# Forward side work of a mixed transformer and state-space kernel: output products, norm and half the gated unit ahead of the input projection

## What is computed

```python
# block 2, per sequence; h is the conditioned norm of x
xz = h @ in_w;  xs, z = split(xz);  xs = silu(xs)
proj = xs @ xproj_w
dt = softplus(proj[..., :512] + dt_bias);  B, C = proj[..., 512:576], proj[..., 576:]
hst = hst * exp(dt[:, None] * A) + (dt * xs)[:, None] * B     # 64 states, over 256 times
y = sum over states of hst * C + xs * Dskip
out_dir = (y * silu(z)) @ out_w                                # once forwards, once backwards
x = x + gate * (h_fwd + h_bwd)
h, gate = conditioned norm of x
return x + gate * ((silu(h @ mlp_w1) * (h @ mlp_w2)) @ mlp_w3)
```

## Time and profile before

| | us |
|---|---|
| median of the runs | 3309.45 |
| profiled execution | 3316.36 |
| its span | 3314.5 |
| PE, DVE, ACT, POOL busy | 3058.3, 2884.0, 2904.8, 2911.3 |

### The profile page before, as it was taken

One profiled execution on the slowest core, in us unless ns is written; L12 is line 12 of the kernel. 1 busy time (PEld: TensorE's weight loads), 2 busy tenths in 40 slices (PEclk: granted clock), 3 DMA queues, 4 the chain that ended last, 5 costly groups with the idle time before them and its releaser, 6 DMA issues.

```text
span 3314.5 us, 71769 instructions
## 1 busy us (share of the span) xinstructions
PE 3058.3 (92%) x23032; PEld 2760.6 (83%) x23032; DVE 2884.0 (87%) x3203; ACT 2904.8 (88%) x6357; POOL 2911.3 (88%) x1552
## 2 busy tenths in 40 slices
PE   8778999999999999999999999999999999998877
PEld 6568988898888988889888898888888898887766
DVE  2269999899989998899998999899988999989985
ACT  1189999898989989899998999899898989989993
POOL 0069999998999999999998999999999999999995
PEclk6699999999999999999999999999999999999998
DMA  5011111111111111111111111112111111111210
GB/s 179 0 42 45 45 46 54 43 52 44 46 51 45 52 44 47 51 50 44 46 54 44 51 45 45 53 45 52 44 47 50 51 46 45 45 50 44 55 47 26
DMA packets 163039, 162.61 MB, mean 49 GB/s; under 512 B 17610, under 2 KB 156874, under 8 KB 162644
## 3 DMA queue, kind: packets, MB, share of 16 engines
q1 hardware_dynamic: 162644, 157.69, 17.5%
HBM read 154.44 MB, written 3.18 MB: 48 GB/s over the span
## 4 chain that ended last, share of the span: by engine, by line
PE 50%; ACT 23%; issue 11%; DVE 8%; POOL 7%; DVEq 0%; ACTq 0%; POOLq 0%; DMA 0%; SPq 0%
PE ps L1263 13%; ACT dA L584 12%; PE ps L1247 12%; ACT uBT L570 6%; PE ps L1010 6%; POOL hst L417 5%; DVE hst L909 5%; PE ps L1245 4%; PE ps L1082 3%; PE ps L1019 3%; PE ps L1057 3%; PE ps L1066 1%; PE ps L1255 1%; PE ps L1131 1%; POOL uBT L430 1%
## 5 line engine op out<-in xcount | busy, mean ns | idle before, releaser
L417 POOL TENSOR_TENSOR hst<-hst,C_sb 128x1024 f32<-128x1024 f32 x1024 | 2447.3, 2407 | 176.1 <-DVE hst L909 172.7
L909 DVE TENSOR_TENSOR_SCAN hst<-dA,ps 128x512 f32<-128x512 f32 x2048 | 2376.7, 1203 | 146.3 <-PE ps L1263 112.9
L584 ACT ACTIVATE dA<-dt,A 128x255 f32<-128x255 f32 x4096 | 1745.0, 501 | 1.4 <-DVE hst L909 1.2
L1263 PE MATMUL ps<-ident,hst 128*128 128x128 f32 x8192 | 1240.7, 274 | 46.8 <-POOL hst L417 46.7
L1247 PE MATMUL ps<-ident,uBT 128*128 128x128 f32 x7104 | 1084.5, 275 | 52.6 <-DVE hst L909 39.8
L570 ACT ACTIVATE uBT<-uT,BT 128x512 f32<-128x512 f32 x1376 | 936.4, 717 | 117.3 <-PE ps L1247 89.2
L1263 PEld LDWEIGHTS ps<-ident,hst 128*128 128x128 f32 x8192 | 963.2, 141 | 62.9 <-POOL hst L417 62.2
L1247 PEld LDWEIGHTS ps<-ident,uBT 128*128 128x128 f32 x7104 | 844.6, 142 | 195.3 <-DVE hst L909 69.4
L430 POOL TENSOR_TENSOR uBT<-uT,BT 128x512 f32<-128x512 f32 x400 | 427.2, 1068 | 1.4 <-PE ps L1245 1.4
L1245 PE MATMUL ps<-uBT,uT 128*128 128x128 f32 x2176 | 302.7, 284 | 33.9 <-DVE hst L909 27.9
L1245 PEld LDWEIGHTS ps<-uBT,uT 128*128 128x128 f32 x2176 | 272.9, 197 | 45.7 <-DVE hst L909 35.9
(11 more groups left out here) (146 smaller groups left out, 2176.0 us busy)
## 6 DMA issues: line engine op xcount, KB each, us to landing
C_sb<-c_dram SPq DMA_DIRECT2D x1024, 128.0 KB, 2.9
gate_l<-gate_rows_dram SPq DMA_DIRECT2D x16, 256.0 KB, 3.8
x_att<-in_x_dram SPq DMA_DIRECT2D x8, 256.0 KB, 3.6
w<-in_L_cond_W_dram SPq DMA_DIRECT2D x2, 1024.0 KB
out_dram<-x_glu SPq DMA_DIRECT2D x8, 256.0 KB, 3.1
wg<-in_L_cond_mlp_w_dram SPq DMA_DIRECT2D x3, 512.0 KB, 11.0
w_xp<-_L_cond_fwd_xproj_w_dram SPq DMA_DIRECT2D x1, 1280.0 KB, 12.5
w_xp<-_L_cond_bwd_xproj_w_dram SPq DMA_DIRECT2D x1, 1280.0 KB, 14.4
```

The lines of the kernel that those rows point to most:

```text
L417: pool.tensor_tensor(h, h, C_sb[:, n % FED:n % FED + 1, :].to_broadcast([P, KI, NB]), ALU.mult).then_inc(hC_ready.sem, 1)
L584: done = act.activation(dA[:, n % NT, c, lo:hi], dt[:, d, c, lo:hi], ACT.Exp, scale=A[:, d, c, n:n + 1])
L909: dve.tensor_tensor_scan(pair(hst[:, n % NR]), pair(dA[:, n % NT]), ps[:, BANK_U + (2 * n + e) % (2 * NU), :][:, way], 0.0, ALU.mult, ALU. ...
L1263: last = pe.matmul(ps[:, BANK_Y + j, c * P:(c + 1) * P], hst[:, n % NR, c, j * P:(j + 1) * P], ident[:, :], start=False, stop=(n == NS - 1 ...
```

## The change

Only the forward pass changes. The order of its side work becomes: post, norm, glu 0 to 4, ins, dts 0 to 13, then glu 5 to 16 with dts 14 to 20 spread among them, dts 21 to 23, first. The silu of the gated unit moves from its own step (with its two table loads) into ins step 10, in front of the two silu operations there; in the tail after the last pass it keeps its own step. The side work starts at h8 instead of h6. The diagonal states of the forward pass move from 22 to 27 to 30 to 35. PE's waits that guard the two shared PSUM banks and the shared tiles follow the new order.

**Where the steps lie after, batches 1 to 6:** post h8 to h16 (transposes h8, DVE copy h9, products h10 to h13, residual h15); norm 0 to 5 h16, h18, h18, h19, h20, h21; glu 0 to 4 h21, h23 to h26; ins 0 to 11 h26 to h38 (step 8 h35, step 10 h36); dts 0 to 13 h38 to h52; glu 5 to 10 h53, h54, h55, h56, h58, h59; glu 11 to 16 h60, h62, h63, h64, h65, h67; dts 14 to 20 h55, h58, h60, h61, h64, h66, h67; dts 21 to 23 h69, h70, h71; first from h72. In batch 0: dts 17 to 20 at h50, h53, h55, h58. In batch 7: dts 17 to 20 at h106, h111, h115, h117, dts 22 at h122.

```diff
--- before.py
+++ after.py
@@ -43,7 +43,7 @@
     NEG = -1e30
     NR = 4
     BEHIND = 3
-    BY_DIAGONAL = ((1, 3, 22, 23, 24, 25, 26, 27, 61, 63), (1, 3, 55, 57, 59, 61, 63))
+    BY_DIAGONAL = ((1, 3, 30, 31, 32, 33, 34, 35, 61, 63), (1, 3, 55, 57, 59, 61, 63))
     by_pool = lambda d, n: n % 2 == 1 and n in BY_DIAGONAL[d]
     by_act = lambda d, n: sum(not by_pool(d, k) for k in range(n))
     FED = 4
@@ -87,10 +87,8 @@
             first = has_next * (stage("first", "norm") + stage("first", "qkv") + stage("first", "heads0") + stage("first", "heads1", 0, HEADS_BEFORE))
             if not has_prev:
                 return stage("own", "ins") + stage("own", "dts") + first
-            return (stage("own", "ins", 0, 10) + meanwhile(stage("last", "post"), stage("own", "ins", 10, 12))
-                    + stage("own", "dts", 0, 2) + meanwhile(stage("own", "dts", 2, 14), stage("last", "norm", 0, 4))
-                    + stage("own", "dts", 14, 17) + stage("last", "norm", 4, 5) + stage("own", "dts", 17, 18) + stage("last", "norm", 5, 6)
-                    + stage("own", "dts", 18, STEPS["dts"]) + stage("last", "glu") + first)
+            return (stage("last", "post") + stage("last", "norm") + stage("last", "glu", 0, 1 + KG) + stage("own", "ins") + stage("own", "dts", 0, 14)
+                    + meanwhile(stage("last", "glu", 1 + KG, STEPS["glu"]), stage("own", "dts", 14, 21)) + stage("own", "dts", 21, STEPS["dts"]) + first)
         if not has_next:
             return stage("last", "post")
         return (stage("first", "heads1", HEADS_BEFORE, STEPS["heads1"]) + stage("last", "post")
@@ -103,7 +101,7 @@
             self.steps = order(d, has_prev, has_next)
             rooms = [self.room(j) for j in range(len(self.steps))]
             self.behind = [[] for i in range(2 * NS)]
-            start = 2 if d == 1 and has_next else FIRST_HALF + 2 * d
+            start = 2 if d == 1 and has_next else 8 + 2 * d
             end = LAST_HALF[d]
             rest = sum(r for r, step in zip(rooms, self.steps) if step[1][:5] != "heads")
             heads = sum(step[1][:5] == "heads" for step in self.steps) + 1
@@ -501,9 +499,12 @@
                         act.preload_act_table_set(LN_EXP)
                     yield
 
-            def prepare(p, d):
+            def prepare(p, d, gated=None):
                 for i in range(STEPS["ins"]):
                     if i == 2 + 2 * KI:
+                        if gated is not None:
+                            act.wait_ge(glu_raw.sem, glu_raw.at(gated, KG))
+                            act.activation(gT[:, :, :], gT[:, :, :], ACT.Silu).then_inc(glu_silu.sem, 1)
                         act.wait_ge(in_raw.sem, in_raw.at(p, KI + TT))
                         act.activation(xsT[:, :, :], xsT[:, :, :], ACT.Silu).then_inc(in_ready.sem, 1)
                         act.activation(sz[:, d], sz[:, d], ACT.Silu).then_inc(in_ready.sem, 1)
@@ -530,9 +531,9 @@
             def post(p):
                 yield from idle(STEPS["post"])
 
-            def glu(b):
+            def glu(b, alone):
                 for i in range(STEPS["glu"]):
-                    if i == 1 + KG:
+                    if i == 1 + KG and alone:
                         act.wait_ge(glu_raw.sem, glu_raw.at(b, KG))
                         act.activation(gT[:, :, :], gT[:, :, :], ACT.Silu).then_inc(glu_silu.sem, 1)
                         act.preload_act_table_set(LN_EXP)
@@ -549,9 +550,9 @@
                 yield from idle(STEPS["down"])
                 yield from norm(b, LN_SSM)
 
-            def close(b):
+            def close(b, alone):
                 yield from norm(b, LN_GLU)
-                yield from glu(b)
+                yield from glu(b, alone)
 
             def forcing(p, d, n):
 
@@ -605,12 +606,12 @@
                 l0 = layer0(b + 1) if has_next else None
 
                 def own():
-                    yield from prepare(2 * b + 1, 1)
+                    yield from prepare(2 * b + 1, 1, b - 1 if has_prev else None)
 
                 def last(b, d):
                     yield from post(2 * b + d)
                     if d == 1:
-                        yield from close(b)
+                        yield from close(b, False)
 
                 def backward():
                     yield from l0
@@ -643,7 +644,7 @@
             period(NBLK - 1, True, False)
             for _ in post(2 * NBLK - 1):
                 pass
-            for _ in close(NBLK - 1):
+            for _ in close(NBLK - 1, True):
                 pass
 
         @block.vector
@@ -1300,14 +1301,14 @@
                     p = 2 * b + d
 
                     def before(j):
-                        if plan.steps[j] == ("last", "post", 0) and d == 0:
-                            pe.wait_ge(in_raw.sem, in_raw.at(p + 1, KI + TT))
                         if plan.steps[j] == ("last", "post", 0) and d == 1 and has_next:
                             pe.wait_ge(o_raw.sem, o_raw.at(b + 1, NG))
-                        if plan.steps[j] == ("last", "norm", 4):
+                        if plan.steps[j] == ("own", "ins", 0) and has_prev:
+                            pe.wait_ge(glu_raw.sem, glu_raw.at(b - 1, KG))
+                        if plan.steps[j] == ("last", "glu", 1 + KG):
                             pe.wait_ge(pre_ready.sem, pre_ready.at(p + 1, KI))
                         if plan.steps[j] == ("own", "dts", 21) and has_prev:
-                            pe.wait_ge(hT_ready[LN_GLU].sem, hT_ready[LN_GLU].at(b - 1, 1))
+                            pe.wait_ge(res_done[RES_GLU].sem, res_done[RES_GLU].at(b - 1, 1))
 
                     return before
 
```

## The result

The changed kernel takes 3334.64 us (median of 4 runs, 3333.51 to 3336.25); the kernel before, run beside it, 3307.43 us. The ratio is 1.0082, interval 1.0063 to 1.0100: the change makes the kernel 27 us slower. The forecast was 3334 us.

What follows compares the result with a forecast made beforehand. Each half-state is set by POOL where side work is thin, PE where dense, DVE at softplus. Six middle passes at +4.5, first +1, last -3 give +25 us on the 3309.45 median: 3334 us, range 3296 to 3351.

Steps and rivals of the forecast that it cites:

- The opening h6 to h15: Start of middle passes: less PE work and POOL finding states earlier gain 3.3 us a pass, bounds 1.5 and 4.
- Sure in sign: Said of the 3.3 us gain a middle pass at h6 to h15: certain to be a gain, bounds 1.5 and 4.
- The norm, h15 to h21: Norm chain with no other chain between: 3.2 us of PE idle time, its work not lost but standing later.
- h22 to h60, PE dense: PE has 59.9 us of work in these halves; 3.3 us of gain are still there at h61.
- The table loads: Two loads fewer in each of seven forward passes: nothing in middle passes, up to 2.6 us each without ACT's cover.
- Softplus, h61 to h71: Three DVE operations meet POOL's multiplications; h72 starts 5.1 us later, 4.5 us a middle pass lost, bounds 2 to 7.
- PE's 15.3 us of h61 to h69: PE's own work there, nine diagonal forcings beside three gated products, said to hide under DVE's softplus stretch.
- The diagonals: Diagonal forcings cost 0.45 us more each: 1.4 us in h22 to h60, nine beside gated products in h61 to h69.
- First and last pass: First forward pass +1 us (-2 to +4), last forward pass -3 us (-6 to +2).
- Near neutral: Rival: DVE operations slip between POOL's; middle pass 0 to +0.5 us, whole 3307 to 3313, say 3310; chance 0.22.
- Faster: Rival: no contention in h54 to h71, the 3.3 us at h61 remain, h72 starts before 1853.5; 3287 us; chance 0.20.
- A falling clock: Rival: PE's hole at h20, h21 or h67 to h69 lowers the clock, 2 to 3 us more a pass; 3350; chance 0.08.

Runs made afterwards that it cites:

- e11_post_first_only: Kernel before with the output products first (h8 to h14), input projection right behind, other steps within one half-state of their old places: 3316.6 us, ratio 1.0021.
- e9_split_norm: Changed kernel with all of dts before glu 5 to 16, softplus at h53 to h59, transposes at h61, diagonal states 27 to 32, norm early: 3327.1 us, ratio 1.0064.
- e3_diag22: Changed kernel with the six diagonal states of the forward pass back at 22 to 27: 3371.3 us, ratio 1.0185.
- e4_own_silu: Changed kernel with the silu of the gated unit back at its own step, with its two table loads: 3344.7 us, ratio 1.0098.
- e10_odd_later: Changed kernel with middle forward passes' softplus operations behind odd half-states (h61, h65, h67, h69) and uT transposes at h71: 3322.9 us, ratio 1.0043.
- e6_split: Changed kernel with all of dts before glu 5 to 16, softplus operations at h53, h55, h57, h59, diagonal states 26 to 31: 3333.7 us, ratio 1.0063.
- e8_before_odd: Kernel before with the four softplus DVE operations of middle forward passes moved to odd half-states h47, h49, h51, h53: 3326.9 us, ratio 1.0044.

## Why the prediction was right, and where it was not

**The time.** 3334 us forecast, 3334.64 measured; +4.5 us a middle pass forecast, +4.4 measured. The sum is right partly by luck, since errors cancel: the scan of h72 was to start 5.1 us later and starts 3.3 later in the mean of the six passes (4.2 in batch 4), and the rest of the pass was to give back 0.6 and loses 1.1.

**The opening h6 to h15.** Forecast 3.3 us, bounds 1.5 to 4. The first sixteen halves are 3.3 shorter in the mean of the six passes (25.7 against 29.0), 2.4 in that of batch 4, and POOL's longest wait there fell from 3.26 to 1.42 us, not to 1 or less. Right in size. "Sure in sign" holds for the stretch, not for the pass: e11_post_first_only has 2.0 of it and keeps none. The prediction itself put PE at full in h22 to h60 and didn't draw the consequence.

**The norm, h15 to h21.** Forecast PE gaps of 1 to 1.5 us and 3.2 in all. Measured a wait of 1.82 us before the first gated product; PE's idle time in h16 to h47 is 2.6 us against 0.6, so 2.0 more. The term was over-sized by 1.2. That it is PE's loss and stands later was right: e9_split_norm, where softplus doesn't wait until h61, takes 1.2 us more than before in h16 to h47 and doesn't get them back.

**h22 to h60, PE dense.** Confirmed by e3_diag22 (4.95 us of work cost 4.95). 3.3 us of gain forecast at h61; the scan of h61 ends 2.5 us ahead in batch 4, 3.4 in the mean of the six passes.

**The table loads.** "Nothing, and up to 2.6 us a pass if that cover were gone." In the changed order, with the silu at its own step, the cover is gone: 1.6 to 2.9 us a pass (e4_own_silu). The duration read from the earlier trace rows, 1.30 us a load, holds: in e4_own_silu the next operation starts 1.29 us behind the first load's start. The Trainium skill's 2.66 us a switch (ScalarE: Activation LUTs, What ACT_TABLE_LOAD costs) is not seen, and isn't needed for this loss.

**Softplus, h61 to h71.** Three collisions forecast, behind h64, h66 and h67, and three measured, at those places. L835 and L839 (now L836, L840) were to take 2.5 to 3.3 us: 2.65 and 2.49, at the lower end. The worked durations of the three, 3.1, 3.7 and 2.4, were too long by 1.8 us together, since POOL, waiting for scans, had less queued than I let it have. The stretch was to take 23 to 24 us: 23.35. e10_odd_later shows the mechanism: without the collisions 2.9 us of it go, 12 us of the whole. PE's 15.3 us of h61 to h69, said to hide under this, were the weakest term: PE is busy 18.6 of the 20.0 us from h61 to h69, 3.3 more than worked out. It does hide, but it takes over as soon as DVE is relieved.

**The diagonals.** The sum counts them where they now lie (1.4 us in h22 to h60, 4.0 in h61 to h69), and nowhere says what the move is worth. Undone alone it costs 37 us, the largest single effect found.

**First and last pass.** First: +1 forecast, -1.4 measured. Last: -3 forecast, -0.5 in the forward and -2.2 in the backward pass behind it. The pass was 11.6 us ahead of before's at h96 and lost 10.2 in h96 to h111 (30.0 us against 19.8), where softplus now stands; its first operation took 8.07 us, behind h106. This collision is not what sets the pass: in e4_own_silu the operation took 4.28 us and the pass 185.1, against 184.8. The prediction had nothing of this.

**The rivals.** Near neutral needed L836 and L840 at 1.2 us; they weren't. Faster needed the scan of h72 before 1853.5 less the pass's start, 113.5 us; it is at 117.7. A falling clock: it didn't fall at the places the rival named, and the granted clock is 1.00 in every stretch of batch 4 behind h16. Its mechanism is real: in batch 3 PE waited 1.17 and 1.65 us at h74 and h76, as in the other five, but there the clock was 0.83 over h74 to h79, and h72 to h127 took 1.0 us more (84.9); in the last pass it was 0.80 in h106 to h111, around a wait of 4.87 us. The length of a wait doesn't decide it alone, as the last section shows.

**Where the loss is made.** Against before: the output products first, +7 us; softplus still by itself but the norm, half the gated unit and the joined silu ahead of the input projection, +21 (with the waits of that edit in it); all of the change, +27; the last with its collisions taken out, +14. The parts don't simply add, since the stretch that pays is PE's in one and DVE's in the other. In batch 4 PE's idle time tells most of it: 6.4 us of the pass before, 10.8 of the changed one (2.0 more around the norm, 2.8 more in h61 to h71 less the 2.0 of h48 to h60, 1.0 more behind h72, 0.7 more in the opening), for a pass that is 5.1 longer. h72 to h127 take 1 to 2.6 us more in all kernels with the new order, of which 0.4 is the heads'. In e9_split_norm the stretch has 3.0 us more of PE's work; in the changed kernel 0.6 us lie in h76 to h79, where ACT is busy 7.45 of 7.59 us. The rest was not settled.

## What to carry to other kernels

Idle time taken out of a stretch is only a gain if the stretches behind it have room; where the engine that did less is full later on, it is postponed work, and what it meets there decides. Before moving an operation of DVE that reads two SBUF tensors, look at what POOL has queued at the new place; and leave the engine that consumes its result, above all PE with its queue in order, other work for the time between. Undoing one part by placing single steps moves their consumers' waits too: read these in the trace of the experiment before its time is put down to the part.

## What the runs showed of the hardware

In all rows looked at, DVE's operations with two SBUF inputs and POOL's exclude one another by whole operations (the Trainium skill, GPSIMD Engine Reference, Specifications, names the contention; the runs agree and give its size), and the one that waits can be passed over more than once: 1.2 us alone, 2.3 to 2.65 behind one multiplication of POOL, 4.12 behind a scaling and a multiplication, 8.07 in the last pass, behind two scalings and two multiplications.

The granted clock can fall after a wait of PE, but the length of the wait doesn't decide it alone. The waits of 1.82 us at the norm left it at 1.00 in all six passes of the changed kernel. In batch 4, waits of 3.37, 4.80 and 5.32 us gave 0.77, 0.84 and 0.72 in the four microseconds around them and 0.80, 0.50 and 0.50 in the next four (1.2 GHz where it is 0.50), and eight transposes took 1.94 us instead of 1.07. But after the wait of 1.96 us in e6_split it fell in four of six passes, after that of 2.32 us in e10_odd_later in three of six, and the 3.69 us of e8_before_odd in batch 3 left it at 1.00.
